# The probabilities turned unsplit, split in the turned copy, and the stack completed by transfers between SBUF rows

## The reference

```python
# h = layernorm(x[b]) (512x512), q = ctx[b] (77x512)
Sim   = (h @ w1)[:, None] + (q @ w2)[None, :] + (h * w3) @ q.T + b_sim   # 512 x 77
A     = softmax(Sim, axis=1)                                             # 512 x 77, "the probabilities"
hq    = A @ q                                                            # 512 x 512
Batt  = softmax(max(Sim, axis=1))                                        # over the 512 rows
hc    = Batt @ h                                                         # one row of 512
x2    = x[b] + concat([h, hq, h * hq, h * hc]) @ W_qv + b_qv             # W_qv 2048 x 512
hid   = layernorm(x2) @ W1 + b1                                          # W1 512 x 2048
act   = relu(hid + c * sin(phase + 0.1 * hid))                           # c, phase: one number per column
out   = x2 + act @ W2 + b2                                               # W2 2048 x 512
```

## Time and profile before

| | us |
|---|---|
| median of 3 runs | 1974.38 |
| lowest, highest | 1972.96, 1977.74 |
| the profiled execution, own time | 1976.23 |
| its span, first to last instruction | 1974.4 |
| TensorE busy | 1946.7 (99%) |
| VectorE busy | 1387.4 (70%) |
| ScalarE busy | 989.3 (50%) |
| GpSimd busy | 389.3 (20%) |
| DMA traffic | 391.73 MB, mean 198 GB/s |

### The profile page before, as it was taken

One profiled execution on the slowest core, in us unless ns is written; L12 is line 12 of the kernel. 1 busy time (PEld: TensorE's weight loads), 2 busy tenths in 40 slices (PEclk: granted clock), 3 DMA queues, 4 the chain that ended last, 5 costly groups with the idle time before them and its releaser, 6 DMA issues.

```text
span 1974.4 us, 24660 instructions
## 1 busy us (share of the span) xinstructions
PE 1946.7 (99%) x8791; PEld 1597.7 (81%) x8791; DVE 1387.4 (70%) x2405; ACT 989.3 (50%) x1676; POOL 389.3 (20%) x834
## 2 busy tenths in 40 slices
PE   7889999999999999999999999999999999999999
PEld 5678788888888888888888888888888888888887
DVE  7777776757767676776767767676776767767554
ACT  5474644636355363654636455363553636446343
POOL 1122212121211212112121121212112121121110
PEclk9999999999999999999999999999999999999999
DMA  8476947667475774847657475774748757475473
GB/s 250 145 264 220 306 147 220 202 190 228 138 237 160 230 216 159 240 132 237 213 175 228 146 222 181 215 223 151 229 136 250 215 166 234 149 220 181 143 218 119
DMA packets 140849, 391.73 MB, mean 198 GB/s; under 512 B 21876, under 2 KB 34856, under 8 KB 138808
## 3 DMA queue, kind: packets, MB, share of 16 engines
q0 software_dynamic: 83568, 304.29, 49.7%
q1 hardware_dynamic: 57016, 85.83, 14.2%
q10 hardware_dynamic: 144, 0.04, 0.0%
HBM read 351.83 MB, written 38.27 MB: 198 GB/s over the span
## 4 chain that ended last, share of the span: by engine, by line
PE 95%; DVE 2%; DMA 1%; ACT 1%; issue 0%; SPq 0%; POOL 0%; DVEq 0%; ACTq 0%; POOLq 0%
PE acc L500 18%; PE acc L502 18%; PE acc L501 18%; PE hid L500 12%; PE hid L502 12%; PE hid L501 12%; PE mis L586 1%; PE mis L509 1%; PE mis L502 1%; PE mis L508 1%; PE acc L509 1%; PE acc L508 1%; PE mis L500 1%; PE mis L501 1%; DMA w_raw<-in_L_ffn_W 0%; DMA w1s<-w1x_dram 0%
## 5 line engine op out<-in xcount | busy, mean ns | idle before, releaser
L500 PE MATMUL hid<-T,w1s 128*128 128x512 f32 x1024 | 404.6, 395 | 9.3 <-DVE w1s L1020 7.5
L500 PE MATMUL acc<-ws,act 128*128 128x512 f32 x1024 | 403.2, 394 | 0.0
L502 PE MATMUL hid<-T,w1s 128*128 128x512 f32 x1024 | 400.2, 391 | 0.0
L501 PE MATMUL hid<-T,w1s 128*128 128x512 f32 x1024 | 399.8, 390 | 0.0
L502 PE MATMUL acc<-ws,act 128*128 128x512 f32 x1024 | 399.8, 390 | 0.0
L501 PE MATMUL acc<-ws,act 128*128 128x512 f32 x1024 | 399.4, 390 | 0.0
L1161 DVE TENSOR_SCALAR kk<-ph 128x512 f32<-128x512 f32 x256 | 108.9, 425 | 331.1 <-ACT ph L842 331.1
L851 ACT ACTIVATE act<-h 128x512 fp32r<-128x512 f32 x256 | 162.0, 633 | 349.4 <-DVE h L1153 328.0
L842 ACT ACTIVATE ph<-hid,hbias 128x512 f32<-128x512 f32 x256 | 175.9, 687 | 286.3 <-PE hid L502 285.9
L1498 POOL DMA_DIRECT2D ws<-w2x_dram x240 | 127.8, 533 | 554.6 <-PE acc L502 545.1
L500 PEld LDWEIGHTS hid<-T,w1s 128*128 128x128 f32 x1024 | 193.1, 189 | 51.7 <-DVE w1s L1020 8.7
(11 more groups left out here) (179 smaller groups left out, 2730.9 us busy)
## 6 DMA issues: line engine op xcount, KB each, us to landing
w1s<-w1x_dram POOLq DMA_DIRECT2D x240, 512.0 KB, 4.0
ws<-w2x_dram POOLq DMA_DIRECT2D x240, 512.0 KB, 4.6
ws<-wqx_dram POOLq DMA_DIRECT2D x56, 512.0 KB, 3.6
full<-in_x_turned SPq DMA_DIRECT2D x15, 1024.0 KB, 8.0
out_x<-X SPq DMA_DIRECT2D x15, 1024.0 KB, 4.7
X<-in_x SPq DMA_DIRECT2D x14, 1024.0 KB, 7.9
w_raw<-in_L_ffn_W SPq DMA_DIRECT2D x32, 256.0 KB, 4.6
w1x_dram<-w1s POOLq DMA_DIRECT2D x16, 512.0 KB, 3.2
```

Of the source, the lines that this page charges most:

```text
L500: pe.matmul(dst, w_hi, m_hi, start=start, stop=False)
L501: pe.matmul(dst, w_hi, m_lo, start=False, stop=False)
L502: mm = pe.matmul(dst, w_lo, m_hi, start=False, stop=stop)
```

## The change

The probabilities are turned as they are: 4 transposes (128 partitions, 77 columns each) instead of 8, in step 6 instead of step 8, and they wait for `prob_done` alone. The two copies of `prob_high` and the two subtractions of `prob_low` are gone. ScalarE makes both copies of high in step 7 (NA - 3), the second from the first after waiting for it. VectorE makes low once, for 77 rows, in step 7, into `at_lo`, a part of `prs`. The rows of low lie in partitions 0 to 76 and belong in others, so two transfers between SBUF rows bring them there: 51 rows and 26 rows of 2 KB. SyncE issues them in step 7, after its other work of that step; in the opening ScalarE issues them. `hq_hat(n, 0)` waits for the transfers, and for `ebc_done` (ScalarE's reading of the bank of `mis` that it writes), as `prob_turn` did.

```diff
-        split_prob = prs[:]...rearrange("p (t k) -> p t k", t=RT)
-        split_high = [split_prob[:, :, 2 * k * J:(2 * k + 1) * J] for k in range(2)]
+        at_lo = prs[0:J, 1, 1]
...
+            def stack_low_in(n):                       # SyncE
+                sp.wait_ge(at_low, n + 1)
+                sp.dma_start(at_s[J:P, 0].bitcast(F32), at_lo[0:JA].bitcast(F32)).then_inc(at_in, 16)
+                sp.dma_start(at_s[J:JB, 1].bitcast(F32), at_lo[JA:J].bitcast(F32)).then_inc(at_in, 16)
...
                     if last:
                         continue
+                    if f == NA - 3:
+                        stack_low_in(n)
...
             def prob_turn(n):                           # TensorE
-                pe.wait_ge(split_lo, 2 * (n + 1))
-                pe.wait_ge(ebc_done, n + 1)
+                pe.wait_ge(prob_done, n + 1)
                 for t in range(RT):
-                    rows = slice(t * P, (t + 1) * P)
-                    pe.transpose(mis[:, 1, rows], split_prob[:, t, 0:P].bitcast(F32), ident[:])
-                    tr = pe.transpose(mis[0:JB, 0, rows], split_prob[:, t, 2 * J:2 * J + JB].bitcast(F32), ident[:])
+                    tr = pe.transpose(mis[0:J, 1, t * P:(t + 1) * P], prob[:, t], ident[:])
                 tr.then_inc(at_done, 1)

             def hq_hat(n, c):
                 if c == 0:
+                    pe.wait_ge(ebc_done, n + 1)
                     pe.wait_ge(at_out, 2 * (n + 1))
+                    pe.wait_ge(at_in if n else at0_in, 32 * max(n, 1))
...
-                    if f == 8 and not last:
+                    if f == 6 and not last:
                         prob_turn(n)
...
-            def prob_high(n):                           # ScalarE
-                sc.wait_ge(prob_done, n + 1)
-                nc.scalar.copy(split_high[0], prob[:]).then_inc(split_hi, 1)
-                nc.scalar.copy(split_high[1], prob[:]).then_inc(split_hi, 1)
             def stack_out(n):
                 sc.wait_ge(at_done, n + 1)
                 need(sc, att_done, RT * n)
-                nc.scalar.copy(at_s[:, 0], mis[:, 1]).then_inc(at_out, 1)
+                nc.scalar.copy(at_s[0:J, 0], mis[0:J, 1]).then_inc(at_out, 1)
+                sc.wait_ge(at_out, 2 * n + 1)
+                nc.scalar.copy(at_s[0:J, 1], at_s[0:J, 0].bitcast(F32)).then_inc(at_out, 1)
+            def first_stack_low_in():                   # the same two transfers, issued by ScalarE, n = 0
+                sc.wait_ge(at_low, 1)
...
                 stack_out(0)
                 high_parts(7)
+                first_stack_low_in()
...
-                    if f == 6 and not last:
-                        prob_high(n)
+                    if f == NA - 3 and not last:
+                        stack_out(n)
                     if f == NA - 1 and not last:
-                        stack_out(n)
                         w0_high(n, 0)
...
-            def prob_low(n):                            # VectorE
-                ve.wait_ge(split_hi, 2 * n + 2)
-                low(split_prob[:, :, J:2 * J], prob[:], split_high[0]).then_inc(split_lo, 1)
-                low(split_prob[:, :, 3 * J:2 * J + JB], ...).then_inc(split_lo, 1)
-            def second_stack_out(n):
-                ve.wait_ge(at_done, n + 1)
-                ve.tensor_copy(at_s[0:JB, 1], mis[0:JB, 0]).then_inc(at_out, 1)
+            def stack_low(n):
+                ve.wait_ge(at_out, 2 * n + 1)
+                low(at_lo, mis[0:J, 1], at_s[0:J, 0]).then_inc(at_low, 1)
...
                         sine_term(g - 1, (f - 1) % FT)
-                    if f == NA - 2 and not last:
-                        second_stack_out(n)
+                    if f == NA - 3 and not last:
+                        stack_low(n)
...
                     if f == 6 and not last:
-                        prob_low(n)
                         row_mean_scale(n)
```

More of the change, by code:

```diff
@@ L130, in xattn_ffn @@
         at_s = sb("at_s", [P, 2, R], F32R)
-        assert 2 * J + JB == 4 * J - JA
-        split_prob = prs[:].rearrange("p a b r -> p (a b r)")[:, 0:RT * (2 * J + JB)].rearrange(
-            "p (t k) -> p t k", t=RT)
-        split_high = [split_prob[:, :, 2 * k * J:(2 * k + 1) * J] for k in range(2)]
+        at_lo = prs[0:J, 1, 1]
         e_bc = sb("e_bc", [P, R])
@@ L207, in xattn_ffn @@
         ebc_done = sem("ebc_done"); erec_done = sem("erec_done"); at_done = sem("at_done")
-        split_hi = sem("split_hi"); split_lo = sem("split_lo"); at_out = sem("at_out")
+        at_out = sem("at_out"); at_low = sem("at_low"); at_in = sem("at_in"); at0_in = sem("at0_in")
         hqh_done = sem("hqh_done"); full_done = sem("full_done")
@@ L880, in stack_out @@
                 need(sc, att_done, RT * n)
-                nc.scalar.copy(at_s[:, 0], mis[:, 1]).then_inc(at_out, 1)
+                nc.scalar.copy(at_s[0:J, 0], mis[0:J, 1]).then_inc(at_out, 1)
[3 more added lines that the diff above has]
+                sc.wait_ge(at_low, 1)
+                nc.scalar.dma_start(at_s[J:P, 0].bitcast(F32), at_lo[0:JA].bitcast(F32)).then_inc(at0_in, 16)
+                nc.scalar.dma_start(at_s[J:JB, 1].bitcast(F32), at_lo[JA:J].bitcast(F32)).then_inc(at0_in, 16)
             def w0_high(n, c):
@@ L911, in attention_first @@
                 row_exponentials(0)
-                prob_high(0)
                 max_exponentials(0)
@@ L1201, in row_mean_scale @@
                 ve.reciprocal(erec[:], esum[:]).then_inc(erec_done, 1)
-            def prob_low(n):
-                ve.wait_ge(split_hi, 2 * n + 2)
-                low(split_prob[:, :, J:2 * J], prob[:], split_high[0]).then_inc(split_lo, 1)
-                low(split_prob[:, :, 3 * J:2 * J + JB], prob[:, :, JA:J], split_high[0][:, :, JA:J]
-                    ).then_inc(split_lo, 1)
-            def second_stack_out(n):
-                ve.wait_ge(at_done, n + 1)
-                ve.tensor_copy(at_s[0:JB, 1], mis[0:JB, 0]).then_inc(at_out, 1)
+            def stack_low(n):
+                ve.wait_ge(at_out, 2 * n + 1)
+                low(at_lo, mis[0:J, 1], at_s[0:J, 0]).then_inc(at_low, 1)
             def row_mean(n, chunks=range(C)):
@@ L1334, in attention_first @@
                 whole_max(0)
-                prob_low(0)
                 row_mean_scale(0)
                 row_mean(0, range(0, 2))
-                second_stack_out(0)
+                stack_low(0)
                 context_low(0, range(1, 2))
```

## The result

| | before | after |
|---|---|---|
| median of 20 runs each, us | 1974.43 | 1978.52 |
| lowest, highest | 1972.96, 1977.74 | 1976.68, 1980.84 |
| span of the profiled execution | 1974.4 | 1978.2 |
| TensorE busy | 1946.7 | 1941.5 |
| ratio, 95% interval | | 1.0019, 1.0013 to 1.0026 |

The account below looks back on a forecast made before the run. From 170 us on TensorE's list of instructions was taken as the bound. Against the profiled 1976.2 us the terms -6.2 + 2.0 + 1.5 + 1.0 = -1.7 gave 1974.5, as a median 1972.7, range 1968.0 to 1979.5.

Parts of the forecast that it names:

- TensorE's saving: Passes 1 to 14: 4 transposes cost 0.44 us less than 8, in sum 6.2 us saved.
- The wait in step 6: Transposes waiting for prob_done: 1.46 us to spare in passes 1 to 14, 0.26 in pass 0; cost 0.
- The new path in the passes: Passes 1 to 14: stack whole 3.1 us after the issue, 5.6 us to spare before hq_hat; cost 0.
- The opening: Transfers on TensorE's path before the first w0 products, landing 3.1 us after issue: +2.0 us, ends +0.8 and +8.8.
- The clock in the opening: TensorE idles 4.5 us before hq_hat(0, 0) and its clock falls behind that: +1.5 us, lower end 0.
- Pass 0: Later release of tile 8 and raw_w1_load(10) behind SyncE's wait for at_low: +1.0 us, ends -0.9 and +3.
- (3): Rival, pass 0: SyncE's wait delays raw_w1_load(10), hidden(10) stalls, up to 5 us late; median 1977 to 1979; chance 0.08.
- (4): Rival, transposes in the passes: 4 cost as much as 8; +4.5 us, 1979; chance 0.02.

Follow-up runs that it names:

- e5: The changed kernel with each of the 4 transposes of step 6 made twice, so 8 again: 1985.47 us, ratio 1.0048.
- e7: Probe on e1: TensorE makes hq_hat(n, 0) at the end of step 8 instead of step 9, so it waits for the transfers in every pass: 2024.44 us.
- e9: The changed kernel with SyncE's first two raw W1 loads held back until the opening's transfers have landed: 1976.55 us, ratio 1.0010.
- e2: The kernel before with the change in the opening alone; passes 0 to 14 as before: 1982.09 us, ratio 1.0033.
- e3: e1 with raw_w1_load(10) issued ahead of SyncE's wait for at_low in pass 0 instead of behind it: 1970.03 us, ratio 0.9970.
- e1: The changed kernel with the opening of the kernel before, so the change in passes 0 to 14 alone: 1971.37 us, ratio 0.9977.
- e10: e3 with raw_w1_load(11) issued ahead of the 1 MB load of x(2) in pass 0 instead of behind it: 1966.87 us, ratio 0.9955.
- e8: e7 with the 51 rows sent as 48 and 3 and the 26 as 16 and 10, four transfers: 2021.48 us.
- e4: The changed kernel with 36 more matmuls on TensorE in the opening's wait for the transfers: 1978.01 us, ratio 1.0012.

## Why the prediction was wrong

- **TensorE's saving**: right. 0.44 forecast, 0.47 measured, 14 times; e5 ties it to the transposes.
- **The wait in step 6**: right. 1.46 us to spare in all passes; in pass 0, 0.26 us were not quite enough, and TensorE waited 0.2 us.
- **The new path in the passes**: right in the outcome, wrong in the number. Nothing waits at hq_hat. But two issues take 1.55 us and not 0.4, and the stack is whole some 5.6 us after the first (by e7), not 3.1. In pass 14 the issue is at 1810.74 and hq_hat at 1819.51, so 3 us were to spare and not 5.6.
- **The opening** is the step that failed. The mechanism was named, the transfers on TensorE's path, and its term was mis-sized: landing 7.7 us after issue for 3.1, so with the 2.87 us of stacked matmuls the w0 products would start at 50.8, +6.3 instead of +2.0. The 3.1 was made of a 36 KB load at the idle start of the kernel (1.9) and 102 KB at the mean rate of another stretch (1.2). It left out ScalarE's issue of 2.1 us for two, the three us until a packet moved, and the second transfer behind the first. "I lean to the low end, since ScalarE's queue holds nothing else" was the choice that decided: an empty queue does not help while the engines behind it are shared (9.9 us in the earlier trace rows), and e9 puts some 1.6 us on that; the larger part, about 6 us, the transfers also take in the passes (e7). The high end of the term, +8.8, would have held it.
- **The clock in the opening**: right. 1.5 us forecast, 2.2 measured; in e2, e5 and e9 the same twelve matmuls lose 1.5 to 1.8. Its premise was weaker than it looked. The 2.2 us wait that was followed by 0.53 before is followed by 1.00 in the changed kernel, e2, e3 and e5. What decides this no run shows. Behind the opening's waits of 6.9 to 8.6 us the clock had fallen in all four traces.
- **Pass 0**: the mechanism was named (SyncE's wait ahead of raw_w1_load(10)), its price too low: +2.9 (2.0 in e1) for +1.0, inside the ends given. e3 brings the stretch back to its old length. The term had no clock in it, and the clock behind the longer wait is a part of the loss (24 matmuls in 8 us for 28). VectorE's later release of tile 8 came as forecast, 0.4 us for 0.5.
- The 1.1 us regained between 44 and 119 us stood in no term. The prediction had TensorE pass on the whole delay; that the change gave them back is not shown, since the stretch has both lengths with either opening.

With the measured terms the sum is -6.5 + 6.3 + 2.2 - 1.1 + 2.9 = +3.8 us. It meets the difference of the two profiled spans because every term was read from the same two traces; e1, e2, e3 and e5 are the test. The measured 1978.52 lies inside the range of 1968.0 to 1979.5, but that is luck: the upper end was drawn from rivals (3) and (4), and no rival had a slow opening. Of the rivals the nearest was (3), SyncE's wait, with 1977 to 1979, but it is not what happened: its share is 2 to 3 us, the opening's is 7 (e2: 6.5).

## What to carry to other kernels

Where a loop hides a transfer, look at the places where it is not hidden: the same edit won 0.47 us in each of 14 passes and lost as much or more in one opening, and making the edit only where it pays (e1) turned a loss into a gain. Price a transfer by one of its own kind, its issue, first packet, number of rows and what shares the engines included, and if the trace has none, let the high end of the range weigh as much as the low one. A queue's list is an order: a wait put into it is paid by the load behind it. Moving 256 KB ahead of that wait gave 1.3 us (e3), which the change had cost, and moving 256 KB ahead of 1 MB another 3 (e10), nearly as much as the change in the passes (3.6). And a wait of TensorE can cost more than its length: look at the granted clock behind it, in more than one execution.

## What the runs showed of the hardware

- 102 KB in 51 rows of 2 KB and 52 KB in 26 rows, between SBUF rows, have both landed 5.6 to 6.3 us after the first issue (e7), and 7.2 to 8.1 us in the crowded opening. 96 KB in 48 rows land after 2.5 us by themselves (e8); with the 29 other rows in three more transfers it is 5.3 to 6.1 us in 14 of 15 passes.
- Issuing one such transfer occupies SyncE's queue for 0.74 to 0.86 us, and ScalarE's for 1.30 and 0.82 us. With the DMA engines full (share 1.03) its first packet moved some 3.1 to 3.3 us after the issue; in pass 14, 1.3 to 1.8 us after it.
- A wait of 8.6 us in which TensorE stood still brought its clock to 1.2 GHz and cost another 2.2 us behind it; filled with matmuls without use, the clock stayed at 2.4 GHz and the landing did not move (47.90, 47.94).
- The same wait of 2.2 us at the same place (for tmp_w) is followed by a granted clock of 0.58 to 0.72 in the kernel before, e1, e4 and e10, and by 1.00 in the changed kernel, e2, e3 and e5: 12 to 14 matmuls in 3.5 us, or 18.
- Four f32 transposes of 128 columns between matmuls add 0.44 us, whether the weights have 128 columns or 77; eight add 0.87.
